# Eight attention batches as straight code or as a loop over pairs, in a transformer layer on one core

## What is computed

```python
q1, q2 = rope(q[..., :32]), rope(q[..., 32:])       # 16 heads; k1, k2 likewise, 4 heads repeated
s1 = einsum('bhtd,bhsd->bhts', q1, k1) * scale + mask
s2 = einsum('bhtd,bhsd->bhts', q2, k2) * scale + mask
diff = softmax(s1) - lam * softmax(s2)
out = einsum('bhts,bhsd->bhtd', diff, v)
out = groupnorm(out) * gn_w + gn_b
x = layernorm(x + out.reshape(B, T, 1024) * (1 - LAMBDA_INIT) @ Wo)
# top 2 of softmax(x @ gate_w.T), weights renormalised
y = sum_e w_e * ((silu(x @ w_gate[e]) * (x @ w_up[e])) @ w_down[e])
x = layernorm(x + y)
```

## Time and profile before

| what | value |
| --- | --- |
| median of 3 runs | 1994.56 us (1994.23 to 1994.79) |
| span of the profiled execution | 1982.6 us, 36940 instructions |
| PE busy | 1681.3 us (85%) |
| PEld busy | 1251.6 us (63%) |
| DVE busy | 1394.1 us (70%) |
| ACT busy | 1166.2 us (59%) |
| POOL busy | 578.0 us (29%) |
| instruction fetches, queues q8 and q14 | 1.06 and 0.70 MB, 0.3% of the DMA engines' time |

### The profile page before, as it was taken

How to read it: one execution, slowest core, us unless ns; L and a number is a source line. 1 busy time by engine, 2 the same in 40 slices (tenths; PEclk the granted TensorE clock), 3 DMA queues, 4 the chain that set the end, 5 groups by cost and what they waited for, 6 DMA issues and landing times. The chain is left out here.

```text
span 1982.6 us, 36940 instructions
## 1 busy us (share of the span) xinstructions
PE 1681.3 (85%) x9718; PEld 1251.6 (63%) x9719; DVE 1394.1 (70%) x3225; ACT 1166.2 (59%) x3388; POOL 578.0 (29%) x471
## 2 busy tenths in 40 slices
PE   4878898898899899889889889873999999999800
PEld 3556556656566655656656665543999999999700
DVE  4998888988888988888898898744333333333377
ACT  2777878877788788787887887832222222222133
POOL 0322322522432432241251252012533342100075
PEclk8999999999999999999999999985999999999955
DMA  8764755765574574484575566014533344433187
GB/s 280 229 169 128 202 139 139 213 170 150 170 202 120 160 207 124 133 232 125 149 229 144 139 203 179 24 71 175 164 118 118 109 127 148 132 95 94 65 258 250
DMA packets 141462, 311.40 MB, mean 157 GB/s; under 512 B 16608, under 2 KB 19296, under 8 KB 140160
## 3 DMA queue, kind: packets, MB, share of 16 engines
q1 hardware_dynamic: 111264, 231.64, 41.3%
q0 software_dynamic: 15072, 50.74, 7.7%
q10 hardware_dynamic: 14976, 27.27, 3.6%
HBM read 207.87 MB, written 101.71 MB: 156 GB/s over the span
## 5 line engine op out<-in xcount | busy, mean ns | idle before, releaser
L856 ACT ACTIVATE expd<-S,neg_max 128x128 f32<-128x128 f32 (+3 forms) x1024 | 530.9, 535 | 152.5 <-DVE neg_max L1042 151.3
L1042 DVE TENSOR_REDUCE neg_max<-S 128x2 f32<-128x768 f32 (+3 forms) x384 | 399.5, 1040 | 144.9 <-PE S L664 135.7
L1073 DVE SCALAR_TENSOR_TENSOR mixed<-expd,rho 128x384 f32<-128x384 f32 (+3 forms) x512 | 338.8, 681 | 0.0
L660 PE MATMUL S<-kT,qT 128*128 128x256 f32 (+2 forms) x1024 | 276.7, 373 | 30.0 <-DMA qT<-parts_rows 18.2
L675 PE MATMUL PTp<-ident,mixed 128*128 128x128 f32 x1280 | 211.7, 280 | 57.4 <-DVE mixed L1073 53.0
L868 ACT ACTIVATE probsT<-PTp 128x512 f32<-128x512 f32 (+2 forms) x384 | 205.2, 534 | 91.3 <-PE PTp L675 88.8
L1529 ACT ACTIVATE xT_hi<-xTp 128x512 fp32r<-128x512 f32 x72 | 43.1, 599 | 357.9 <-DVE yo L1710 352.0
L660 PEld LDWEIGHTS S<-kT,qT 128*128 128x128 f32 x1024 | 162.5, 193 | 132.5 <-issue 92.0
L722 PE MATMUL tail<-wo,ctxT 128*128 128x512 f32 x464 | 218.9, 595 | 0.3
L856 ACT ACTIVATION_READ_ACCUMULATOR expd<-S,neg_max 128x1 f32 x1024 | 216.7, 212 | 0.0
L555 POOL TENSOR_TENSOR swapped<-swapped,rope_t 128x512 f32<-128x512 f32 x77 | 99.1, 1287 | 397.2 <-DVE swapped L1035 397.2
(11 more groups left out here) (245 smaller groups left out, 3632.7 us busy)
## 6 DMA issues: line engine op xcount, KB each, us to landing
qT<-parts_rows SPq DMA_DIRECT2D x256, 256.0 KB, 4.5
parts_rows<-parts SPq DMA_DIRECT2D x160, 256.0 KB, 2.8
wqk<-wqk_split SPq DMA_DIRECT2D x75, 512.0 KB, 6.1
xin<-expert_in_rows SPq DMA_DIRECT2D x72, 256.0 KB, 3.0
expert_out_rows<-yo ACTq DMA_DIRECT2D x72, 256.0 KB, 3.2
kT<-parts_rows SPq DMA_DIRECT2D x64, 256.0 KB, 4.2
x<-in_x SPq DMA_DIRECT2D x8, 1024.0 KB, 7.2
x_rows<-x SPq DMA_DIRECT2D x8, 1024.0 KB, 7.3
```

The lines of the kernel that those rows point to most:

```text
L660: nc.tensor.matmul(S[s % 2][:, k * slot:k * slot + w], qT[kv % 2][:, 2 * h + c, i * P:(i + 1) * P], kT[kv][:, c, 0:w], start=(k % per_bank ...
L856: ex = nc.scalar.activation(expd[s % 3][:, k * slot:k * slot + w], S[s % 2][:, k * slot:k * slot + w], ACT.Exp, bias=neg_max[s % 3][:, k:k ...
L1042: nc.vector.tensor_reduce(neg_max[s % 3][:, 0:k], v, AX, ALU.max, negate=True).then_inc(max_ready, 1)
L1073: ins = nc.vector.scalar_tensor_tensor(out=mixed[sl % 3][:, a * 256:a * 256 + w], in0=e2, scalar=rr[:, i, h:h + 1], in1=e1, op0=ALU.mult, ...
```

## The change

The helper `batches` loses its loop and its parameter for the engine, and the three engines call it without. All eight batches of PE, ACT and DVE are Python calls of the same `body` with the same arguments (batch number, parity, whether first or last), so the order of the steps is unchanged and b is a plain number everywhere. SP's and POOL's loops stay, as do the loops of the experts and of the combine.

```diff
-        def batches(eng, body, end):
-
-            body(0, 0, True, False)
-            with eng.Fori(0, (B - 2) // 2) as m:
-                for r in (1, 0):
-                    body(m * 2 + 2 - r, r, False, False)
-            body(B - 1, (B - 1) % 2, False, True)
+        def batches(body, end):
+
+            for b in range(B):
+                body(b, b % 2, b == 0, b == B - 1)
             end(B)
...
-            batches(nc.tensor, body, end)
+            batches(body, end)
...
-            batches(nc.scalar, body, end)
+            batches(body, end)
...
-            batches(nc.vector, body, end)
+            batches(body, end)
```

## The result

The changed kernel takes 1984.01 us (median of 6 runs, 1976.26 to 1986.36), the kernel before beside it 1994.06 us (6 runs). The ratio is 0.9937, 95% interval 0.9916 to 0.9958. A second measurement with 12 runs, against 30 of the kernel before, gave 1985.36 against 1993.31 us, ratio 0.9950, interval 0.9930 to 0.9971. The intervals are those of the ratios: taken times the median beside them they give a gain of 12.6 us (8.4 to 16.8) and of 10.0 us (5.8 to 14.0), while the medians themselves are 10.05 and 7.95 us apart. The change is faster by 0.5 to 0.6%: some 10 us where 7.5 were forecast, with some 4 us of doubt on either side.

What follows compares the result with a forecast made beforehand. The prediction took attention's ring of PE, DVE and ACT as the bound, where uncovered stalls delay everything after. Span 1982.60 - 6.9 (branches, exit) - 0.6 (registers) = 1975.1, plus 11.96 outside, gave 1987.1 us; range 1981.5 to 1991.

Steps and rivals of the forecast that it cites:

- The two branches: Attention's loop, after batches 2 and 4: taken backward branches stall DVE while code is fetched; removing them gains 6.83 us.
- DVE's stall covers PE's: At both branches: DVE's stall is the longest and hides PE's (2.06 us at the first), so PE's is not added.
- nothing is given back later: Within a batch after a stall: 26 steps take 82.04 us, against 81.98 without one, so the whole stall counts.
- The registers: Batches 1 to 6: waits and addresses become constants; gain taken as 0.6 us, bounds 0 and 2.6 us.
- The comparison over 26 steps: First 26 steps of batch 3 (registers) against batch 7 (constants), 82.04 and 81.98 us; basis for 0.1 us per batch.
- the ring: Attention's cycle of scores, maxima, exponentials, mix and transposes over PE, DVE and ACT, turning 48 times per batch.
- The time outside the span: Whole kernel: median 1994.56 us less profiled span 1982.60 us leaves 11.96 us, kept unchanged in the forecast.
- a measurement tells 0.2% from no change: Whole kernel: a time 4 us faster, below 1990.6 us, was taken as distinguishable from no change.
- TensorE's clock: Five half-clock stretches in batches 3 to 6, costing 5.5 us; effect taken as 0, bounds -5.5 and +3.4 us.
- rivals 1 and 2: Attention's clock falls: all gone, 1981.6 us, chance 0.10; or two more, 1990.5 us, chance 0.09.
- rival 1: Attention: the clock falls vanish too, 5.5 us more gain, 1981.6 us; chance 0.10.
- Rivals 3 and 4: Stalls stay or return elsewhere, 1993.9 us, chance 0.07; experts' loop refetches at 33 branches, 2043 us, chance 0.03.

Runs made afterwards that it cites:

- before_again: The kernel before, unedited, run again for a second profile and more times; ratio 0.9998 to other runs of the same kernel, profiled run 1995.61 us.
- pe_act_out: Against the kernel before, PE's and ACT's batches written out, DVE alone left in the loop; one run, 1994.95 us.
- dve_out: Against the kernel before, only DVE's batches written out, PE and ACT left in the loop; ratio to before 0.9982.
- dve_registers: Against the changed kernel, DVE's batch number made a register value again in batches 1 to 6, without loop or branch; ratio to before 0.9952.
- after: The changed kernel in its first measurement and profile; 1984.01 us, ratio to before 0.9937.
- after_again: The changed kernel, unedited, run again for a second profile and more times; ratio to before 0.9950.
- sp_loads: Against the changed kernel, the combine's 64 GpSimd gathers replaced by 64 plain SyncE loads of the same size; 1959.54 us, ratio to before 0.9822.
- one_gather: Against the changed kernel, one gather per token tile in the combine instead of two; 1957.56 us, ratio to before 0.9811.

## Why the prediction was right or wrong

**The two branches.** Right in mechanism and size. Forecast 6.83 us; the traces of DVE in the loop give 6.8, 6.4 (`before_again`) and 6.1 (`pe_act_out`). The argument that DVE's stall covers PE's is shown by `pe_act_out` and `dve_out`. The reason given, that DVE's is the longest, is not right: from branch to target PE loses 3.6 us and DVE 3.6 at the first, 3.8 and 3.0 at the second, but PE branches 3.9 us earlier and has work queued; DVE's stall is the one that ends last. That nothing is given back later is shown by the 47 steps of a quiet batch, 153.1 to 153.3 us in every kernel. The Trainium skill (Advanced Engine Details and Errata, Control Flow Timing) gives a compare-and-branch about 108 ns. That is near the price of the branch not taken, 0.1 to 0.2 us here, and of the near one (0.2 us from branch to target), not of the far one. The runs side with the Trainium skill's page Runtime: NRT & Kernel Launch, Instruction fetch mechanics, by which a branch to a target that is not loaded waits for its fetch: far or near is what counts.

**The registers.** This is the step that failed, a term of the sum that was mis-sized: 0.6 us forecast, 2.0 measured (`dve_registers`). The step is "The comparison over 26 steps is the nearest row, so I take 0.1 us per batch". The 26 steps do not hold the seam, and the 0.32 us were at the seam. Their rows had the full answer, and so had the sentence that DVE is next to be late there. The fear that the ring would swallow it had no row behind it, and the seams of 3.47 us show that the ring did not swallow it.

**The time outside the span.** "11.96 us lie outside the span" was wrong: it is 1.8 us by the other traces, and the rest was the distance of one short execution from a usual one. It moved no term of the difference, so the time of 1987.1 us suffered nothing by it. But it hid the spread from run to run, and with it was wrong the statement that a measurement tells 0.2% from no change: three runs that agreed within 0.6 us were taken for the kernel's spread, and 30 runs span 19 us.

**TensorE's clock.** That stretches of half clock come and go was right, and that the sum's centre is 0. But they do so between executions of one kernel: batch 4 lasts 162.92 us in the first profile of before, of which the forecast put 3.1 us down to the clock, and 161.17 in the second; batch 6 lasts 158.45 and then 156.92, with no half clock left in it, and batch 1, quiet at first, 157.28 and then 158.92. Batches 3 and 4 of the second profile:

```profile
511.71:668.40 156.69, 143.89 (x855) 97.25 (x854) 137.70 (x323) 125.71 (x377) 47.97 (x41) 1.00 0.59 167
668.40:829.57 161.17, 146.20 (x853) 98.59 (x852) 137.73 (x324) 125.69 (x377) 52.19 (x45) 0.98 0.59 166
```

So falls come and go without any change, and no trace shows that the change adds or takes any: rivals 1 and 2 were spread and not cases of the change.

**The sum, redone.** Seams 27.7, 27.3 and 27.0 us in the three traces with DVE in the loop, 18.8 with all written out: 8.2 to 9.0 us, against 7.5 forecast and 10 measured with 4 us on either side. Batches 1 to 6 as a whole say the same: 951.8 us in the mean of these three traces, 943.5 in that of the four of kernels with all three engines written out and plain numbers (`after`, `after_again`, `sp_loads`, `one_gather`), 8.3 us less. The runs can't tell 8.2 from 10, and the 7.5 us of the forecast lie inside the interval of the second measurement (5.8 to 14.0) and below that of the first (8.4 to 16.8). The median of 1984.01 us lies in the range of 1981.5 to 1991; the ratio of 0.9937 applied to the time beside it gives 1981.5, just at its lower end. That it lies no lower is luck: the range reached so far down for rival 1, the 5.5 us of the clock, which is no effect of the change. Rivals 3 and 4 did not happen: no new issue stall of DVE, at the seams or within the batches, none of PE over 0.3 us there (its weight loads aside, which have none over 1.0), and the experts' loop takes 485.5 us in the trace before and 485.6 in the one after. SyncE's and GpSimd's loops, left as they are, cost nothing.

## What to carry to other kernels

Look for "issue" idle time that comes as often as a hardware loop branches back: here a body of two batches paid 2.4 to 3.9 us at each backward branch on each engine, while the experts' loop of two tiles shows no such stall. The engine's stall that ends last covers the others, so every engine whose stall would come to light must be rid of it. The branch's own records, under the loop's line, show the stall and who has it. Register-made waits and addresses cost nothing that shows where an engine has work queued, and about 0.3 us in a chain in which it waits for its own last results; find the row of just that place and don't average it away. Before a profile's span is subtracted from a median, compare it with the time of that same execution, and take the spread from more than three runs.

## What the runs showed of the hardware

DVE can start 2 us behind its own result while GpSimd issues gathers. In the kernel after, the statistics of L1841 wait, by the program, for nothing but the sum of L1836 just ahead of them on the same engine ("remote" is the profile's word for what released them):

```profile
1932.75 0.75 DVE L1836 SCALAR_TENSOR_TENSOR res<-ya,wts,res 128x512 f32<-128x512 f32 x1 [1.15 <-issue]
1933.42 0.15 DVE L1850 RECIPROCAL rs<-sd 128x1 f32<-128x1 f32 x1
1935.54 0.69 DVE L1841 BATCH_NORM_STATS2 bs<-res 128x6 f32<-128x512 f32 x1 [1.96 <-remote]
```

In the same time GpSimd issues gathers, one every 1.26 us as a rule, 1.50 between these two:

```profile
1933.14 1.19 POOL L1784 DMA_INDIRECT ya<-expert_out_rows,out_slots  x1 [0.30 <-issue]
1934.64 0.95 POOL L1784 DMA_INDIRECT ya<-expert_out_rows,out_slots  x1 [0.30 <-issue]
```

The sum ends at 1933.50 and the statistics start 2 us later. This is rare: in this trace 28 of the 32 statistics start within 0.04 us of the end of their sum, and four in a row start 0.7, 2.0, 2.1 and 1.3 us behind it; in the first trace of before, with its combine of 104 us, all 32 start within 0.04. So it goes with the long combines and makes up part of their spread. The 20 to 32 us that the combine is shorter without the gathers are something else for the most part: in the short combine of before DVE waits 21.6 us for gathered rows to land, in `sp_loads` 3.3.

```profile
DVE res L1834 <- DMA ya<-expert_out_rows,out_slots: 21.6, 19, 5.5
...
DVE res L1830 <- DMA ya<-expert_out_rows: 3.3, 1, 3.3
```

Whether it is the way to SBUF, the descriptors or the counting of semaphores that holds DVE up was not tried, and stays open. The Trainium skill (SBUF — State Buffer, Who interferes with whom) says that a DVE instruction with two inputs in SBUF contends with a GpSimd instruction that reads SBUF. L1836 has two such inputs, L1841 has one, and it is L1841 that comes late; L1836 is late as well in this trace, but its length stays 0.75 us.

At a far branch the first instruction at the target starts 3.5 to 3.9 us after the branch on PE, 2.8 to 3.6 us on DVE and 2.4 to 2.8 us on ACT. PE works off what is queued meanwhile, so that it idles 2.25 us of them, and ACT's add nothing to the kernel's time.
